# A fused attention, MLP and quantised linear kernel: Q's products moved ahead of the first gather, and one layer norm's statistics split round another product

## What is computed

```
x1 = x + L(LN(x))                      # L: the layer below
    y  = LN(x)
    n  = LN(y)*g1 + b1 ; q = n@wq ; k = n@wk ; v = n@wv      # 16 heads of 16
    fq = elu(q)+1 ; fk = elu(k)+1
    kv = sum over the sequence of fk^T v ; z = sum of fk
    y2 = y + ((fq@kv) / (fq.z + 1e-6)) @ wo
    L  = y2 + gelu_on_a_grid_of_0.1( (LN(y2)*g2 + b2) @ w1 ) @ w2
out = x1 + (LN(x1) @ CB^T) * SCB/127 + bias
```

## Time and profile before

| | |
|---|---|
| median of 3 runs | 575.92 us (574.35 to 576.08) |
| profiled execution, its own time | 573.73 us |
| its span in the profile | 571.9 us |
| PE busy | 536.6 us, 94% |
| PE weight load busy | 486.8 us, 85% |
| DVE busy | 448.7 us, 78% |
| ACT busy | 394.7 us, 69% |
| POOL busy | 348.5 us, 61% |
| mean granted TensorE clock | 0.99 of full speed |
| HBM traffic over the span | 51 GB/s |

### The profile page before, as it was taken

How to read it: one execution, slowest core, us unless ns; L and a number is a source line. 1 busy time by engine, 2 the same in 40 slices (tenths; PEclk the granted TensorE clock), 3 DMA queues, 4 the chain that set the end, 5 groups by cost and what they waited for, 6 DMA issues and landing times.

```text
span 571.9 us, 11318 instructions
## 1 busy us (share of the span) xinstructions
PE 536.6 (94%) x3610; PEld 486.8 (85%) x3610; DVE 448.7 (78%) x1059; ACT 394.7 (69%) x656; POOL 348.5 (61%) x336
## 2 busy tenths in 40 slices
PE   6799999999999899999999999999999999999895
PEld 6788888788887789889898898988989899898775
DVE  5789889789776587888878878787886978879636
ACT  2386785555567686877768787687876968768760
POOL 3343444325143467687877868768687786877654
PEclk9799998999999999999999999999999999999999
DMA  8421221121001010110102101021010101100001
GB/s 272 134 74 63 85 73 39 37 74 37 22 19 57 1 37 24 51 68 5 73 0 73 54 21 74 0 73 40 34 73 0 73 37 37 73 0 37 38 1 76
DMA packets 11419, 29.47 MB, mean 52 GB/s; under 512 B 2048, under 2 KB 4864, under 8 KB 11392
## 3 DMA queue, kind: packets, MB, share of 16 engines
q1 hardware_dynamic: 9472, 28.32, 13.6%
q10 hardware_dynamic: 1920, 0.79, 0.7%
HBM read 20.71 MB, written 8.39 MB: 51 GB/s over the span
## 4 chain that ended last, share of the span: by engine, by line
PE 59%; DVE 20%; issue 10%; ACT 5%; POOL 4%; DMA 2%; DVEq 0%; ACTq 0%; POOLq 0%; SPq 0%
PE psum L1028 54%; PE psum L1046 4%; DVE bn_stats_b L690 3%; DVE bn_stats L690 2%; DMA f_arena<-in_L_attn_x_dram 2%; DVE f32r_arena L843 2%; POOL f32r_arena L383 2%; DVE n_and_ones L717 2%; DVE f32r_arena L835 2%; DVE mean_var L697 1%; DVE phi_q L741 1%; ACT f_arena L501 1%; DVE f_arena L736 1%; ACT psum L524 1%; DVE f32r_arena L725 1%
## 5 line engine op out<-in xcount | busy, mean ns | idle before, releaser
L1028 PE MATMUL psum<-w_hi,f32r_arena 128*128 128x256 f32 x1280 | 174.3, 282 | 4.7 <-POOL f32r_arena L383 3.0
L1028 PEld LDWEIGHTS psum<-w_hi,f32r_arena 128*128 128x128 f32 x1280 | 164.0, 188 | 14.2 <-issue 5.9
L1028 PE MATMUL psum<-f32r_arena,w_hi 128*128 128x512 f32 x512 | 141.1, 403 | 0.8 <-issue 0.8
L383 POOL TENSOR_TENSOR f32r_arena<-f_arena,f32r_arena 128x512 fp32r<-128x512 f32 x64 | 85.9, 1343 | 82.1 <-ACT f32r_arena L620 46.0
L607 ACT ACTIVATE grid_index<-psum,w_bias_in_steps 128x512 int8<-128x512 f32 x128 | 87.0, 680 | 47.3 <-PE psum L1028 47.2
L1028 PEld LDWEIGHTS psum<-f32r_arena,w_hi 128*128 128x128 f32 x512 | 88.1, 188 | 14.2 <-issue 1.0
L618 ACT ACTIVATE f_arena<-grid_index 128x512 f32<-128x512 int8 x128 | 80.8, 632 | 24.9 <-POOL f32r_arena L383 16.5
L620 ACT ACTIVATE f32r_arena<-grid_index 128x512 fp32r<-128x512 int8 x128 | 79.2, 619 | 0.0
L1028 PE MATMUL psum<-f32r_arena 128*128 128x256 f32 (+1 forms) x384 | 68.0, 333 | 1.9 <-DVE f32r_arena L729 1.9
L1028 PEld LDWEIGHTS psum<-f32r_arena 128*128 128x128 f32 x384 | 58.3, 196 | 8.2 <-issue 2.1
L835 DVE TENSOR_TENSOR f32r_arena<-f_arena,f32r_arena 128x512 fp32r<-128x512 f32 x64 | 57.2, 893 | 3.0 <-ACT f32r_arena L620 3.0
(11 more groups left out here) (117 smaller groups left out, 874.5 us busy)
## 6 DMA issues: line engine op xcount, KB each, us to landing
f_arena<-in_L_attn_x_dram SPq DMA_DIRECT2D x32, 512.0 KB, 3.3
out_dram<-f_arena SPq DMA_DIRECT2D x15, 512.0 KB, 2.6
f_arena<-in_L_attn_w_dram SPq DMA_DIRECT2D x2, 1024.0 KB, 12.5
out_dram<-f_arena SPq DMA_DIRECT2D x2, 256.0 KB, 2.1
phi_q<-in_L_attn_wk_dram ACTq DMA_DIRECT2D x1, 256.0 KB, 4.5
phi_q<-in_L_attn_wq_dram SPq DMA_DIRECT2D x1, 256.0 KB, 4.7
phi_q<-in_L_ffn_CB_dram SPq DMA_DIRECT2D x1, 256.0 KB, 7.1
phi_q<-in_L_attn_wo_dram SPq DMA_DIRECT2D x1, 256.0 KB, 7.4
```

What stands on the lines that cost most here:

```text
L383: nc.gpsimd.tensor_tensor(t_lo[m % SLOTS], tf[m % 2], t_hi[m % SLOTS].bitcast(F32), ALU.subtract).then_inc(s["t_lo_p"], 1)
L1028: return nc.tensor.matmul(out_, lhs, rhs, start=start, stop=stop, skip_group_check=True)
```

## The change

In phase 1, `query(c)` moves on PE from behind `gather(c, 1)` to just behind `turn1(c+1)`, ahead of `gather(c, 0)`. With it ACT's `q_exps` and `q_relus` and DVE's `phi_query` treat chunk c in the same turn instead of chunk c-1: ACT's exp and relu stand together behind `gain1(c+1)`, and `phi_query(c)` takes the place of `phi_query(c-1)`. The three calls behind the loop that did the last chunk go.

In phase 2, DVE's four bn_stats of `xp` are cut in two: two stay ahead of `attn_low(i+1)`, and the other two, with the four bn_aggr, go behind it.

```diff
             # ACT, pair
-                    if past(c, 1):
-                        q_exps(c - 1)
                     k_pair(c, 0)
...
-                    if past(c, 1):
-                        q_relus(c - 1)
+                    q_exps(c)
+                    q_relus(c)
...
-            q_exps(CHUNKS - 1)
-            q_relus(CHUNKS - 1)
             # DVE
+            def half_sums3(h):
+                for j in (2 * h, 2 * h + 1):
+                    i = ve.bn_stats(bn_b[:, 6 * j:6 * j + 6], tm(xp)[:, j])
+                if h == 1:
+                    i.then_inc(s["bn3"], 1)
...
                 if prv:
                     v.wait_ge(s["xp_ready"], c + 1)
-                    sums(xp, bn_b, "bn3")
-                    mean_var(i - 1, bn_b, mv3, "bn3", "mv3_ready")
+                    half_sums3(0)
...
                 if nxt:
                     attn_low(i + 1)
+                if prv:
+                    half_sums3(1)
+                    mean_var(i - 1, bn_b, mv3, "bn3", "mv3_ready")
...
-                    if past(c, 1):
-                        phi_query(c - 1)
+                    phi_query(c)
...
-            phi_query(CHUNKS - 1)
             # PE, pair
                             turn2(0)
+                        query(c, p)
                         gather(c, p, 0)
...
                         gather(c, p, 1)
-                        query(c, p)
```

## The result

The changed kernel takes **585.73 us** (median of 4 runs, 583.92 to 589.54), the kernel before 575.13 (574.2 to 576.08) beside it: ratio 1.0188, 95% interval 1.0146 to 1.023. It is slower by 10.6 us, as forecast in sign; the forecast of 583.0 is 2.7 too low. The profiled execution took 586.07, its span is 584.3, against 573.73 and 571.9 before.

What follows compares the result with a forecast made beforehand. PE, busy 94% of the span, was taken as the bound. Phase 1's -4.7 and phase 2's +13.0 sum to +8.3: 582.0 on the profiled 573.73 us, 584.2 on the median 575.92; forecast 583, range 573 to 590.

Steps and rivals of the forecast that it cites:

- forecast A: Phase 2: late `normalise`, low part held by POOL's addition, `down(i, 3)` +0.93 in 14 iterations; 576.5 to 589 us; chance 0.66.
- Rival C: Phase 2: `normalise` late, but L835 not or only half held behind POOL's addition; 573 to 579 us; chance 0.13.
- Rival B: Phase 2: the hole at `attention_out` closes and nothing takes its place; 560 to 562 us; chance 0.12.
- Rival D: Phase 1 gives nothing either, as a margin breaks; with phase 2's +13, 588 to 592 us; chance 0.09.
- two tight margins: Phase 1, chunks 1 to 7: Q's loop 8.11 against PE's 8.12 us; norm done 0.2 us before the turn.
- The lock: Phase 2: DVE's low part L835, blocked by POOL's addition, ends 0.55 us after POOL.
- The added 0.13 per iteration: Phase 2: if blocked L835 ran its whole 0.68 behind POOL, 0.13 us more per iteration, 1.8 in all.
- The other hold that the forecast had: Phase 2: POOL's L362 and DVE's L835 both read SBUF, one waits; L362 ends about 304.28, `normalise` 1.25 us late.
- Behind it PE had no hole; all it does shifts: Phase 2, PE behind `down(i, 3)`: all later work shifts with its delay, 14 x 0.93 = +13.0 us.
- -4.7 forecast: Phase 1 together: -3.7 - 1.1 + 1.5 - 1.2 + 0.2 - 0.4 us, bounds -9 and +1.
- the same work in another order ...: 0: Phase 1, chunk 8: same work reordered, DVE's key sums in front, 0 us.
- Chunk 9's queue on DVE: Phase 1, chunk 9: `blocks` waits for the turned sums' copy behind DVE's queue, +1.5 us, between 0 and +2.4.

Runs made afterwards that it cites:

- the half addition: Changed kernel with POOL's phase 2 addition of residual and output bias covering only half of the columns: 576.37 us.
- the half dose: Changed kernel's phase 1; in phase 2 all four bn_stats, then only the first of two attention low parts ahead of bn_aggr: 568.9 us.
- the first part: Changed kernel with the phase 2 split undone, so only Q's products move in phase 1: 570.66 us, ratio 0.9898 to the kernel before.
- The split's own time: Kernel before with only phase 2's statistics in two halves, phase 1 as before: 589.56 us, ratio 1.0214.
- the early copy in chunk 9: Phase 1 move alone, plus DVE's copy of the turned key sums right behind the flag in chunk 9: 571.07 us in one run.
- the edits of phase 2: Added to phase 1's edits: `up(i, 4)` ahead of `attention_out`, and the low part for `down(i, 3)` between the residual's bn_stats and bn_aggr: 567.99 us.

## Why the prediction was right, and where its sizes were off

**The sign and the mechanism of forecast A hold at each step.** `attention_out` without a wait; `normalise` 1.31 late (forecast 1.25); the low part's end at +12.63 (forecast 311.25 - 298.66 = +12.59); `down(i, 3)` at +12.69 (forecast +12.64). The experiments confirm its two halves apart: lateness alone makes the wait, and a shorter addition on POOL takes the hold away. Rival C (no hold) falls by the half addition. Rival B's condition was that `normalise` be less than 0.3 late; the half dose shows that such a point exists, but the split is past it. Rival D falls: phase 1 gives 5 us by itself. One of its two tight margins did break, though, in chunk 8 (below).

**The lock.** The forecast took 0.55 from the end of POOL's instruction to the end of the blocked one; the traces show 0.54 and 0.55. The Trainium skill's rule ("SBUF — State Buffer", section "SBUF: two separate sides") agrees in kind. The added 0.13 per iteration, if the blocked one had to run its full 0.68, isn't seen. The other hold that the forecast had, of POOL's L362 by DVE's low part, shows too: 0.43 instead of 0.20.

**The size of the iteration's loss: +0.93 forecast, +1.11 measured.** This is the term that carries the error, 14 x 0.18 = 2.5. The step that failed is "Behind it PE had no hole; all it does shifts". Of the 0.18, 0.05 stands at `down(i, 3)`'s start; the group behind it starts 1.05 later and not 0.94, 0.11 more. A wait of PE costs more than its length, and I counted lengths.

**Phase 1: -4.7 forecast, -3.6 in the changed kernel's trace.** The loop of chunks 1 to 7 came out at 8.11, PE's own work of 8.12, and not my 8.15: no margin broke there. Chunks 10 to 13 gave 2.0 and not 1.2. The step that failed is chunk 8, "the same work in another order ...: 0". It cost 2.4 in that trace and 0.8 in four others. The forecast's own margin says why: the norm needs 0.4 + 1.38 behind the gathers and has K's products, 1.97, before the turn. In chunk 8 only half of them, 0.98, stand ahead of the turn, so the 0.2 of room is a lack of 0.8. In the trace the norm started 0.56 behind K's first product (83.97), straight behind a `phi_query` that had waited 0.26 for ACT's relu, and PE's turn came 1.0 late. The order of `turn1` in the listing of the kernel would have shown it. The rest of the 2.4 is the slow stretch behind the one-column matmuls, which was there before and was longer in this trace. The kernel before shows it in a row that the forecast didn't take in:

```profile
96.20 5.40 PE L1028 MATMUL psum<-n_and_ones,f_arena 128*128 128x257 f32 x16
```

That is the gather behind the bias, 5.40 long where the earlier trace rows has 3.74. Chunk 9's queue on DVE was right, with +1.0 inside its bounds of 0 and 2.4. Chunks 14 and 15 and iteration 0 gave +0.5 and +0.4 where I had -0.2 and 0; these weren't followed up.

By the first part's own time (-5.0) the forecast of -4.7 was good, in part by luck: in the changed kernel's trace chunk 8 (+2.4) and chunks 14 and 15 (+0.7) went against it, and chunks 0, 1 to 7, 9 and 10 to 13 gave 2.0 more than it had. The split's own time (+13.9) is 0.9 above its +13.0. By both, the whole was low by the iteration's term; the other 1.7 of the +10.6 is within what these medians can tell. Rival D's upper end of 592 has no term behind it: +14 gives 588 to 590.

## What to carry to other kernels

A wait at the top of PE's list is worth closing only if what is moved aside has slack. Here a 128x4 statistic was moved back, whose consumer sits one round trip through POOL away. Some 0.3 of its lateness was absorbed, the rest was paid for one to one, with 0.13 to 0.16 on top. Half of the move, one low part ahead of bn_aggr instead of two, made the norm 0.10 late and cost nothing, but it gained nothing clear either (23.92 per iteration against 23.97). Ask of a late instruction which long instruction of a port-sharing engine it will now meet. Count a wait of PE as the distance between the starts of its neighbours, not as the idle time shown. A margin found in a loop must be read again at each place where the order is written out differently, as in chunk 8.

The two parts belong apart: the first alone gives 570.66. With Q's products ahead of the bias in chunk 8 and the early copy in chunk 9 it is 568.35, but the ratios to the kernel before, 0.9898 and 0.9863, have intervals that overlap. With the edits of phase 2 it is 567.99, the lowest median here, 8.2 below the kernel before and 17.7 below the changed one (which ran in another group). The medians from 567.99 to 568.9, the half dose's, can't be told apart.

## What the runs showed of the hardware that was not expected

- A wait shown as 0.15 to 0.16 ahead of a group of fp32 matmuls cost 0.41 to 0.43 over the next two starts, and such a wait stands in each of 14 iterations; one shown as 0.64 cost 0.80. 0.16 of each is how idle time is counted.
- Of what ran on DVE during POOL's 2.4 us addition, only the low part, with two SBUF operands, was held (0.66 became 1.34). The four bn_stats that started round its start and ran on beside it took 1.40 as ever, and so did the residual addition from PSUM beside POOL's L383 (1.21). The hold goes the other way too: POOL's L362, which started while DVE's low part ran, took 0.43 instead of 0.20.
- Within and behind 32 matmuls of one column the granted clock fell in every trace, to between 0.50 and 0.82 in a stretch of 5 us; with 4 of them, in one run, it stayed at 1.00. The same code had a chunk of 15.1, 16.7 or 18.4 us by it.
